# A first projection spread over the first attention, and a re-ordered output stage, in a two-block transformer kernel

## The reference, cut to what matters

```
x = layernorm(x + attention0(x))   # tanh-squashed scores plus two feature terms
x = layernorm(x + ffn0(x))         # int4-rounded kernel, bias, low-rank term
x = layernorm(x + attention1(x))   # rotary embedding, plain softmax
x = layernorm(x + ffn1(x))         # token shift, relu squared, sigmoid gate
```

## Time and profile before

| | |
|---|---|
| runs, median (lowest to highest) | 4131.27 us (4129.25 to 4133.75), 3 runs |
| profiled execution, its time / its span | 4128.27 us / 4125.7 us |
| PE / ACT / DVE / POOL busy over the span | 90% / 84% / 63% / 10% |
| mean granted TensorE clock | 0.981 |

### The profile page before, as it was taken

How to read it: one execution, slowest core, us unless ns; L and a number is a source line. 1 busy time by engine, 2 the same in 40 slices (tenths; PEclk the granted TensorE clock), 3 DMA queues, 4 the chain that set the end, 5 groups by cost and what they waited for, 6 DMA issues and landing times. The chain is left out here.

```text
span 4125.7 us, 61470 instructions
## 1 busy us (share of the span) xinstructions
PE 3703.2 (90%) x21943; PEld 1418.7 (34%) x21958; DVE 2592.8 (63%) x4548; ACT 3478.9 (84%) x2950; POOL 425.9 (10%) x407
## 2 busy tenths in 40 slices
PE   6978989989999989999889699969999999999787
PEld 2432323223323223323223366622222222222565
DVE  5647888788887788887788476633232323232688
ACT  2429999999999999999999566659999999999233
POOL 3540000000000000000000055510000000000232
PEclk9989999999999999999999899979999999999899
DMA  5862121111121111111121377632222222121331
GB/s 163 263 205 66 46 61 46 40 54 58 50 61 43 40 57 56 52 58 43 38 62 33 101 187 198 159 101 76 76 71 71 79 62 82 59 82 40 117 93 47
DMA packets 272882, 339.63 MB, mean 82 GB/s; under 512 B 39054, under 2 KB 206062, under 8 KB 272305
## 3 DMA queue, kind: packets, MB, share of 16 engines
q1 hardware_dynamic: 272564, 335.58, 27.7%
HBM read 207.18 MB, written 128.25 MB: 81 GB/s over the span
## 5 line engine op out<-in xcount | busy, mean ns | idle before, releaser
L842 DVE SCALAR_TENSOR_TENSOR att_prob<-att_tanh,alpha,ps 128x512 f32<-128x512 f32 x2176 | 1506.5, 740 | 410.3 <-ACT att_tanh L786 366.6
L726 PE MATMUL ps<-att_q,att_k 99*128 99x512 bf16 (+5 forms) x5120 | 1134.3, 350 | 114.8 <-DMA att_v<-v_ones 57.3
L755 PE MATMUL ps<-att_prob,att_v 128*32 128x512 f32 (+3 forms) x10240 | 1162.2, 540 | 2.0 <-ACT att_prob L795 1.9
L786 ACT ACTIVATE att_tanh<-ps,rbeta 128x2048 f32<-128x2048 f32 x544 | 1125.7, 2069 | 36.0 <-PE ps L726 36.0
L795 ACT ACTIVATE att_prob<-att_prob 128x2048 f32<-128x2048 f32 x544 | 1095.7, 2014 | 1.5 <-DVE att_prob L842 1.3
L792 ACT ACTIVATE att_prob<-ps 128x1024 f32<-128x1024 f32 x1088 | 1054.4, 1021 | 25.5 <-PE ps L726 9.5
L736 PE MATMUL ps<-att_f,att_g 75*128 75x512 bf16 (+3 forms) x2560 | 810.4, 354 | 133.4 <-DVE att_prob L842 121.6
L726 PEld LDWEIGHTS ps<-att_q,att_k 96*128 96x128 bf16 (+1 forms) x5120 | 399.2, 98 | 962.4 <-ACT att_prob L792 427.0
L831 DVE TENSOR_TENSOR att_prob<-att_prob,keep 128x512 f32<-128x512 f32 (+1 forms) x320 | 187.4, 586 | 580.2 <-ACT att_prob L792 579.2
L736 PEld LDWEIGHTS ps<-att_f,att_g 75*128 75x128 bf16 x2560 | 231.7, 96 | 927.9 <-DVE att_prob L842 906.9
L755 PEld LDWEIGHTS ps<-att_prob,att_v 128*32 128x32 f32 x10240 | 216.2, 108 | 347.7 <-ACT att_prob L792 142.0
(11 more groups left out here) (143 smaller groups left out, 2690.2 us busy)
## 6 DMA issues: line engine op xcount, KB each, us to landing
att_v<-v_ones SPq DMA_DIRECT2D x128, 256.0 KB
att_k<-k_parts SPq DMA_DIRECT2D x128, 192.0 KB
att_q<-q_parts SPq DMA_DIRECT2D x128, 192.0 KB
v_ones<-proj_vs SPq DMA_DIRECT2D x64, 256.0 KB, 3.8
att_k<-k_parts SPq DMA_DIRECT2D x128, 128.0 KB
att_q<-q_parts SPq DMA_DIRECT2D x128, 128.0 KB
o_t<-att_on SPq DMA_DIRECT2D x512, 32.0 KB, 1.7
v_ones<-mid_vs SPq DMA_DIRECT2D x64, 256.0 KB, 3.3
```

Source lines behind the costliest of these rows:

```text
L726: mm = pe.matmul(ps[:, bank, col:col + w], keys, q_s[:, n % QU, h, q0:q0 + w], start=True, stop=True)
L755: mm = pe.matmul(ps[VW * h:VW * (h + 1), O0 + n % 2, q0:q0 + w], v_s[:, c % KU, kb % CB, h * VW:(h + 1) * VW], prob[:, S % R, h, col:col + ...
L786: th.done(act.activation(tanh_s[:, S % 2], ps[:, QK0:QK0 + HQ], ACT.Tanh, scale=kn["rbeta"][:, 0:1]))
L842: sc.done(dve.scalar_tensor_tensor(prob[:, S % R, h], tanh_s[:, S % 2, h], kn["alpha"][:, 0:1], ps[:, E0 + h % 2], ALU.mult, ALU.add))
```

## The change: where the projection runs, and the order of the output stage

`project_phase` of layer 0 runs for sequence 0 alone. The 12 groups of sequences 1 to 3 are projected inside the first attention, one group in each of the sets 0 to 11 (NX = 12, NU = 9 units: seven tiles and two halves of v). Each unit's matmuls are cut into pieces of one 256-column f32 matmul (512 columns for the g unit), put at 15 of the 34 steps of a set, none of them masked: place `a` is after `extra(S,1)` and ahead of `scores(S+1)`, place `b` between `extra(S,2)` and `extra(S,3)`. The units use the output banks 6 and 7 at times when attention doesn't.

The g unit is taken out of its bank by a tanh on ScalarE, between tanh(S) and exp(S-1) of the step after its last piece. The other eight are copied out by VectorE ahead of the first `sums` instruction of the very step that holds the last piece, and for q, k and f GpSimd makes all three parts from that copy:

```
+            def evict(j):
+                X, kind, m, tile, n, bank = unit(j)
+                if kind == "v":
+                    bg_ps.wait(dve, j)
+                    v_out.wait(dve, m, X - 1)
+                    bg_ev.done(dve.tensor_copy(vs[:, m, :, :, 0:HD], ps[:, bank].rearrange("p (t h d) -> p t h d", t=2, h=H)))
+                elif kind != "g":
+                    bg_ps.wait(dve, j)
+                    low.wait(dve, tile - 2)
+                    bg_ev.done(dve.tensor_copy(raw[0:n, tile % 2], ps[0:n, bank]))
...
                 for h in range(HQ):
+                    if h == 0 and unit_at(S) is not None:
+                        evict(unit_at(S))
                     if h == 2:
                         normalise(due, 1)
...
+                for j in range(NX * NU):        # GpSimd, four operations to a tile
+                    hi.done(pool.tensor_copy(parts[0:n, u, 0], src))
+                    rest.done(pool.tensor_tensor(rem[0:n], src, parts[0:n, u, 0], ALU.subtract))
+                    mid.done(pool.tensor_copy(parts[0:n, u, 1], rem[0:n]))
+                    low.done(pool.tensor_tensor(parts[0:n, u, 2], rem[0:n], parts[0:n, u, 1], ALU.subtract))
```

SP's queue in both attentions is ordered by step: loads of a group four steps after the last step of the group whose slot they take, stores of a unit five steps after it, stores of an output seven. In the first attention the four weight arrays and two groups of x are loaded between the first and the second stack load:

```
+            for n in range(QU):
+                load(n)
+                if layer == 0 and n == 0:
+                    for name, t in (("wq", wq_s), ("wk", wk_s), ("wv", wv_s), ("w12", w12_s)):
+                        sp.dma_start(t[:], w[name]).then_inc(w_in, 16)
+                    load_x(0)
+                    load_x(1)
```

The branch for row maxima gets the missing projections too, but it is not taken with these inputs. In the output stage TensorE's order becomes y of i, k, r and v of i-1, transposes of i; both norms' scalings go to ScalarE (`apply_act`); only Wo, and o and x of group 0, are loaded ahead of the rest:

```
+            pe.wait_ge(wo_in, 16)
+            for i in range(NG + 1):
...                # y(i); k, r, v of i-1; transposes of i
+            for i in range(NG + 4):            # ScalarE, g = i - 1, e = i - 3
+                if has(e):
+                    n2.take_root(act, e, e % 2, kn["eps"][:, 0:1])
+                    n2.apply_act(act, e, e % 2, lambda t: x4[:, e % 2, t], lambda t: rr2[:, e % 2, t])
...                # relu of g
+                if has(i):
+                    n1.take_root(act, i, i % 2, kn["eps"][:, 0:1])
+                    n1.apply_act(act, i, i % 2, lambda t: x3[:, i % QU, t], lambda t: rr[:, i % 2, t])
...                # sigmoid of g, copies of i
+            for i in range(NG + 4):            # VectorE, g = i - 1, f = i - 2, e = i - 3
...                # gate of f; edge and k-mix of g; inverse of e; r-mix of g;
...                # sum and statistics of i; sum of f; inverse of i; statistics of f
```

More of the change, by code:

```diff
@@ L628, in attend_phase, with pieces, unit_at, unit @@
     QK0, E0, O0 = 0, 4, 6
+    tiles = [("g", 0), ("q", 0), ("q", 1), ("k", 0), ("k", 1), ("f", 0), ("f", 1)]
+    NTL = len(tiles)
+    kinds = tiles + [("v", 0), ("v", 1)]
+    NU = len(kinds)
+    NX = (B - 1) * GB if layer == 0 else 0
+    plan = ["9a 9b", "12a 12b 12b 13a", "13b 14a 14b 15a", "15b 16a 16b 19a", "24a 24b 24b 25a", "25b 26a", "26b 27a", "27b 28a 28b 29a", "29b 30a 30b 31a"]
+    slots = {}
+    for u, places in enumerate(plan):
+        places = places.split()
+        for i, p in enumerate(places):
+            slots.setdefault(p, []).append((u, i, i == len(places) - 1))
+    bank_of = {u: O0 + (1 if 1 <= u <= 3 else 0) for u in range(NU)}
+    behind = {0: 0, 1: 1, 4: 2}
+    ahead = {2: 0, 3: 3, 0: 8}
+    def pieces(S, place):
+        it, s = divmod(S, NST)
+        return [(it * NU + u, i, last) for u, i, last in slots.get(f"{s}{place}", [])] if 0 <= it < NX else []
+    def unit_at(S):
+        ended = [j for j, i, last in pieces(S, "a") + pieces(S, "b") if last]
+        return ended[0] if ended else None
+    def unit(j):
+        X, u = divmod(j, NU)
+        kind, m = kinds[u]
+        return X, kind, m, X * NTL + u, {"q": P, "k": P, "f": 96, "g": NF, "v": P}[kind], bank_of[u]
     SR, FR = (QROWS, FROWS + 3) if layer == 0 else (QROWS + 3, 0)
@@ L753, in weigh @@
                         o_tr.wait(pe, n - 2)
+                        X = it - 1 if g == 0 else it
+                        if g in ahead and 0 <= X < NX:
+                            bg_ev.wait(pe, X * NU + ahead[g])
                     for h in range(HQ):
@@ L779, in _, with feature @@
                 c.start(act)
+            def feature(j):
+                X, kind, m, tile, n, bank = unit(j)
+                if kind == "g":
+                    bg_ps.wait(act, j)
+                    if X >= 2:
+                        low.wait(act, tile - 2 * NTL)
+                    bg_ev.done(act.activation(f12[:, X % 2], ps[0:NF, bank], ACT.Tanh))
             for S in range(N + 1):
@@ L935, in _ @@
                 if layer == 0:
+                    with act.Fori(0, B - 1) as b:
+                        for gq in range(GB):
+                            act.wait_ge(tile_ps, b * NTB + gq * NTL + 1)
+                            act.activation(f12[:], ps[0:NF, 3], ACT.Tanh).then_inc(feat, 1)
                     with act.Fori(0, B * NHQ) as it:
@@ L1486, in _ @@
                 sp.dma_start(dst[:], src).then_inc(w_in, 16)
-            for gq in range(GB):
-                load(sp, 0, gq)
+            load(2)
             out.start(sp)
-            def do(step, b, gq, g):
-                if step == "load":
-                    if b + 1 < B:
-                        r1.wait(sp, g * 2 + 1)
-                        load(sp, b + 1, gq)
-                else:
-                    n2.out.wait(sp, g)
-                    out.done(sp.dma_start(rows(out_d, b, gq), x4[:, gq % 2]), gq % 2)
@@ L1501, in _ @@
-            over_groups(sp, ("0load", "3store"), do)
+            for i in range(NG + 4):
+                if has(i + 3):
+                    r1.wait(sp, (i - 1) * 2 + 1)
+                    load(i + 3)
+                if has(i - 3):
+                    n2.out.wait(sp, i - 3)
+                    out.done(sp.dma_start(rows(out_d, i - 3), x4[:, (i - 3) % 2]), (i - 3) % 2)
             for u in range(2):
-                out.wait(sp, u, B * GB // 2 - 1)
+                out.wait(sp, u, NG // 2 - 1)
@@ L1647, in _ @@
+                if has(f):
+                    for half in range(2):
+                        rv.wait(dve, f * 2 + half)
+                        r2.done(dve.tensor_tensor(rr2[:, f % 2, two(half)], rr2[:, f % 2, two(half)], x3[:, f % QU, two(half)], ALU.add))
+                if has(i):
+                    n1.invert(dve, i, u)
+                if has(f):
+                    n2.take(dve, f, f % 2, lambda t: rr2[:, f % 2, t], lambda t: r2.wait(dve, f * 2 + t // 2))
         @block.gpsimd
```

404 lines of the change are left out of this document (280 added, 124 removed).

## The result

The changed kernel takes 4103.31 us (median of four runs, 4100.62 to 4105.59) against 4130.26 for the kernel before on the same chip: a ratio of 0.9934 [0.9918, 0.9950]. It is faster by 27 us where the prediction's terms add up to 115, and outside the range given. The profiled execution spans 4098.8 us, 26.9 less than before.

| part | before | after | change | forecast |
|---|---|---|---|---|
| up to the first tanh | 305.57 | 133.53 | -172.0 | -173 |
| first attention | 1989.85 | 2147.22 | +157.4 | +80 (4 + 76) |
| the rest | 1830.27 | 1818.00 | -12.3 | -22 |

A forecast was written before the change was run, and what follows sets the result against it. ScalarE was taken to bound the first attention, TensorE the first projection. 4128.3 - 173 + 4 + 76 - 22 = 4013.3 us, with 3.0 for the median 4016; range 3940 to 4085.

The forecast's parts named there:

- What bounds the kernel: First attention: ScalarE busy 1869 of 1870 us; VectorE work beyond 0.6 us in a step is paid in full.
- The projection, -173: First projection: removing 12 groups, which take 172.97 us, saves 173.0 us; the stage's start and drain stay.
- The start, +4: Start of first attention: weights and x between the stack loads cost 4 us, between 2 and 10.
- Pieces on TensorE: First attention: 256-column pieces nearly free at 0.43 us each; g unit 0.4 plus its tanh 0.55 a set.
- The copies on VectorE: First attention: eight copies of projected units delay the sums, 5.4 us a set; with the g unit +76 in all.
- Zero: First attention: GpSimd's new operations and SP's added DMAs stay covered and cost nothing.
- the step that weighed the rule: First attention: sums have one PSUM operand, so GpSimd, sharing VectorE's second SBUF read interface, costs them nothing.
- GpSimd's and SP's other work: Both attentions: 16 more DMAs a set leave stack loads hidden; second attention keeps its waits; zero.
- The output stage, -22: Output stage: period 15.76 in place of 17.05 us gives -19; start -4, last group's scalings +0.7.
- Nothing hidden: Rival 2, first attention: TensorE is the bound, its added work bare, 166 in place of 76; 4106 us, chance 0.18.
- Hidden: Rival 1, first attention: copies start earlier or sums have more room; attention pays 7 + 4; 3947 us, chance 0.18.
- Slower: Rival 3, first attention: GpSimd's work stretches VectorE's sums from 0.69 to 1.14 us; 4189 us, chance 0.04.

The follow-up runs named there:

- experiment 2: Changed kernel with GpSimd's four operations on a tile working on one column in place of 512: 4057.74 us, ratio 0.9822 to the kernel before.
- experiment 5: Changed kernel with the due part of `normalise` ahead of VectorE's copy in steps with a copy, GpSimd's work whole: 4059.32 us against 4129.32 for the kernel before.
- experiment 9: Changed kernel with each unit's last piece at place b and its copy ahead of the next step's first sum: 3961.52 us against 4131.27 for the kernel before.
- experiment 11: Changed kernel with the f units' matmuls over 128 rows, 116 of them zeros, in place of 12: 4067.03 us, ratio 0.9845 to the kernel before.
- experiment 4: Changed kernel without TensorE's pieces but for one one-column matmul a unit, copies and GpSimd kept: 4011.92 us, ratio 0.9715 to the kernel before.
- experiment 3: Changed kernel with GpSimd's operations and VectorE's copies of the units both on one column: 4020.94 us, ratio 0.9737 to the kernel before.
- experiment 6: Changed kernel with each unit's copy behind the first sum of its step, not ahead of it: 4018.16 us, ratio 0.9716 to the kernel before.
- experiment 8: Changed kernel with VectorE's edge column ahead of the gate in the output stage: 4096.93 us, ratio 0.9926 to the kernel before.

## Why the prediction was wrong, point by point

**What bounds the kernel.** Right for the kernel before: ScalarE sets the pace of the first attention, and what exceeds VectorE's 0.6 us is paid in full.

**The projection, -173.** Right: -172.0. **The start, +4.** Right: tanh of step 2 waits 5.71 us, before 2.67, and set 0 lengthens by 3.6 more than the others.

**Pieces on TensorE.** Right in the main. Step 19, alone in its stretch, has exp(S) at 5.90 after tanh(S), forecast 5.8. The g unit costs 0.27 + 0.52 = 0.8 a set in steps 9 and 10, forecast 0.95.

**The copies on VectorE: the step that failed.** I had 5.4 us a set; without a fall it is 134.9 - 124.3 - 0.8 = 9.8. Over twelve sets that is 53 of the 77 us by which the attention missed. Two errors are in it:
- GpSimd stood at "Zero". For the sums that was right: 741 ns, 740 before. But the step that weighed the rule looked at the sums alone, while the same paragraphs had named, for u1 and u4, "a product of 0.42 from `normalise`", an op with two SBUF inputs. It meets GpSimd there and takes 1.36: 2 x 0.9 = 1.8 a set (experiments 2 and 5: 1.8 and 2.2). The rule of the Trainium skill that I had quoted covers exactly this op; "SBUF — State Buffer", section "SBUF: two separate sides", adds that whichever starts first holds the shared ports for its whole instruction. The trace agrees: GpSimd's subtraction starts at 1015.45 and ends at 1016.61, and the product, begun at 1015.52, ends at 1016.88; in set 8, where the product starts first, it isn't slowed.
- The rest, about 2.6 a set, is the copy's start. I took most steps by themselves, and carried lateness over in full only in steps 26 and 27. In step 13 it comes over from the transpose of step 11 through step 12: the piece ends late, the copy waits 1.21 us, and the sums wait behind it. Steps 13 to 16 cost 3.2 a set, forecast 1.55, and steps 25 to 28 4.7 without a fall, forecast 3.15; of both misses 0.9 is the product. The larger part of the rest is v: steps 29 to 32 cost 1.7, forecast 0.1 + 0.3. Both v units have a b piece in the step before their copy, which I had counted for u1 and u4 and not for them: v0's copy starts 2.89 after tanh, not 2.38. Step 19, which has no such piece before it, costs 0.4, forecast 0.3.

**TensorE's clock: not in the sum.** Seven falls of 3.9 us are 27 of the 77 (the g unit gives 2 back). In the changed kernel they vanish, all or most, with either of two changes: with shorter stalls there are one or two (experiments 2 and 5), with the order of experiment 9 none, and with the stalls kept and 128 rows none either (experiment 11). In general neither is shown to be needed: experiment 4 has low stretches without the 12-row pieces, and experiments 3 and 6, with shorter stalls, have three and five falls. Which sets fall isn't fixed by the code. The attention of experiment 8 is the changed kernel's, and its trace has falls in sets 0, 1, 3, 4, 6, 7, 9 and 11. What decides it stays open.

**GpSimd's and SP's other work.** Right: TensorE waits for stacks four times, as before, at the starts of the two attentions (57.3 us in all before, 61.2 now; the 4 more are the start's), and sets 12 to 15 take what they took.

**The output stage, -22.** The direction was right, the size not: 12. The period fell by 1.00, not 1.29 (the sum of the prediction's own 4.6 and 0.7 is 5.3, not 5.35, which alters little): the part of ScalarE's 3.35 us that sticks out, taken as 0.7, is 1.06 (transposes to k 5.71, forecast 5.35), and experiment 8 shows where half a microsecond of it was: in the edge behind the gate. The last k now has 23.3 us to the end, 20.1 before, since the pipeline is one group deeper: +3.2, where I had +0.7. The first k comes 1.4 later after the first y, for which I had nothing. The wait for o fell from 15.13 to 12.2, 3 us of the 4, but in this execution the stages ahead of it took 2.9 longer, so the first y comes no earlier after the first attention than before (1528.7 us after its last tanh in both). The traces of these runs differ by up to 5 us in that stretch.

**The rivals.** "Nothing hidden" gave 4106, next to the measured 4103, and is nevertheless wrong: experiment 9 has the same matmuls and copies and takes 3961.5. TensorE was not the bound; it waited, 8% of the time. It held ScalarE's tanh up where the clock had fallen, by 2.78 us in step 27 of set 6; this sign of that rival did show, from another cause. "Hidden" (3947) did not happen in this kernel, but it is nearly what the work costs when it is placed well: 125.9 a set, 1.6 over the kernel before. "Slower" rested on sums at 1.14 us; they stayed at 0.74. What it feared happened to the product.

The range ended at 4085, in the lower half of that rival, and its upper bound was the bare time of TensorE's work, 13.8 a set. Waits that engines cause each other are not bounded by the work of one: a set with a fall takes 138.8 - 124.3 = 14.5 more.

## What to carry to other kernels

An instruction that waits for another engine belongs, in an in-order queue, behind the work that has nothing to wait for: the same work cost 10.6 us a set with each copy in the step of its last piece, and 1.6 with each a step later and the pieces rearranged for it (4.1 with the copy merely behind one sum, experiment 6). Before work on GpSimd is called free, look through VectorE's whole queue of that stretch for an op with two SBUF inputs, not only at the op that is on the path. And when a price depends on what the step before left late, follow the chain in time over the neighbouring steps before adding up steps one by one.

## What the runs showed of the hardware

- A product of 0.42 us on VectorE (two SBUF inputs, 256 columns) took 1.36 when it started 0.07 us after a GpSimd subtraction of 1.16 us with two SBUF inputs, and 0.42 when it started 0.21 ahead of one. In the output stage the sum of two SBUF inputs (L1892) took 0.68 us with GpSimd idle, and 1.40 to 1.53 when it started 0.18 us or more after GpSimd's square; it had 0.69 in the order before (L1638), where none met GpSimd. VectorE's sums with one operand in PSUM had a mean of 741 ns with GpSimd's work beside them, 740 without.
- GpSimd's f32 to bf16 cast of 128x512 took 0.61 us, its subtraction with two inputs 1.16; I had assumed 0.89 and up to a third more. VectorE's copy of a 128x512 tile out of PSUM took 0.69.
- Matmuls over 12 of 128 rows, in stretches with stalls, stood beside a granted clock of 0.51 (1.2 GHz) in seven sets of eleven; the same count and columns over 128 rows, 116 of them zeros, beside 1.00 in all. Doubling the 12-row ones did not help: all twelve sets had a fall. TensorE had been busy 6.29 of 8 us ahead of a fall in set 6, 6.29 in set 4, where none came, and 5.92 in experiment 11, where none came either, so its busy time in the profile does not tell them apart.
